# A first stage with maxima as b + relu(a - b) on row tiles, and a second attention with keys on partitions

## The reference

```
x = x + xattn(layernorm(x), ctx)      # ctx: 8192 keys; rope by position ids on q and k; softmax over 8192 keys
x = x + attn(layernorm(x))            # causal over the 512 latents; pairs (2i, 2i+1) rotated by position * frequency
x = x + moe(layernorm(x))             # 32 experts of 128, top 4 by softmax of the router, and 4 blocks of a shared expert
```

## Time and profile before

| | us |
|---|---|
| runs | 1833.15, 1833.43 and 1842.78; median 1833.43 |
| profiled execution | 1837.42, its span 1835.8, mean granted clock 0.965 |
| first stage, start to its last maximum | 0 to 726.2 |
| pass over all keys | 735 to 1316 |
| second attention's projections to its output projection | 1349.2 to 1501.6 |
| experts and the end | 1520 to 1835.8 |
| transfers, median from issue to landing | `kh<-kscr` 4.1, `qe<-vscr` 4.8, `cs<-kr` (swap) 6.3 |

### The profile page before, as it was taken

How to read it: one execution, slowest core, us unless ns; L and a number is a source line. 1 busy time by engine, 2 the same in 40 slices (tenths; PEclk the granted TensorE clock), 3 DMA queues, 4 the chain that set the end, 5 groups by cost and what they waited for, 6 DMA issues and landing times.

```text
span 1835.8 us, 21316 instructions
## 1 busy us (share of the span) xinstructions
PE 1686.4 (92%) x8556; PEld 1142.7 (62%) x8556; DVE 1357.2 (74%) x1095; ACT 839.8 (46%) x1083; POOL 686.4 (37%) x323
## 2 busy tenths in 40 slices
PE   5489999999999996998999999999985998999998
PEld 4377777777777773433444344434564986888886
DVE  5579899999999998999999898898752563222222
ACT  3312222222222210977888888888731654333332
POOL 3266655566665653998000000000040004444432
PEclk8789999999999998998999999999997999999999
DMA  4634445334445327543455545444339003343431
GB/s 150 202 115 149 154 165 164 126 126 149 150 168 161 106 92 190 138 115 93 111 120 123 120 118 124 115 115 115 96 95 265 20 1 115 122 131 122 132 121 57
DMA packets 73905, 231.62 MB, mean 126 GB/s; under 512 B 8924, under 2 KB 9180, under 8 KB 62992
## 3 DMA queue, kind: packets, MB, share of 16 engines
q1 hardware_dynamic: 72768, 227.39, 42.8%
q10 hardware_dynamic: 1040, 2.88, 0.6%
HBM read 150.45 MB, written 59.84 MB: 115 GB/s over the span
## 4 chain that ended last, share of the span: by engine, by line
PE 54%; POOL 17%; DVE 10%; DMA 8%; ACT 5%; issue 5%; SPq 1%; POOLq 0%; ACTq 0%; DVEq 0%
PE PS L585 12%; PE PS L617 10%; PE PS L113 8%; PE PS L114 8%; PE PS L115 7%; DMA cs<-kr 6%; POOL kr L453 4%; POOL cs L451 4%; POOL kr L450 4%; POOL kl L464 4%; PE PS L371 3%; DVE acc L608 2%; DVE mpart L375 2%; PE PS L893 2%; ACT P L591 2%
## 5 line engine op out<-in xcount | busy, mean ns | idle before, releaser
L375 DVE TENSOR_REDUCE mpart<-PS 128x2 f32<-128x1024 f32 x512 | 584.8, 1219 | 61.2 <-PE PS L371 61.1
L608 DVE TENSOR_TENSOR acc<-acc,P 128x2048 f32<-128x2048 f32 x216 | 508.5, 2417 | 34.9 <-ACT P L591 34.9
L591 ACT ACTIVATE P<-PS 128x1024 f32<-128x1024 f32 x512 | 481.5, 1039 | 97.8 <-PE PS L585 75.6
L371 PE MATMUL PS<-kh,Qbd 128*128 128x512 f32 x1024 | 326.5, 401 | 24.0 <-ACT kh L462 12.7
L617 PE MATMUL PS<-P,qe 128*32 128x512 f32 x2048 | 259.8, 606 | 0.7 <-ACT on L622 0.7
L371 PEld LDWEIGHTS PS<-kh,Qbd 128*128 128x128 f32 x1024 | 192.5, 192 | 81.9 <-DVE mpart L375 20.9
L108 POOL TENSOR_TENSOR w3l<-qk,w3h 128x2048 fp32r<-128x2048 f32 x2 | 9.1, 4557 | 481.7 <-ACT w3h L105 481.7
L108 POOL TENSOR_TENSOR El<-We,Eh 128x1536 fp32r<-128x1536 f32 x36 | 126.0, 3501 | 166.3 <-ACT Eh L105 166.3
L450 POOL TENSOR_TENSOR kr<-kr,cs 128x512 f32<-128x512 f32 x64 | 82.4, 1287 | 233.6 <-DMA cs<-kr 233.6
L1040 DVE TENSOR_TENSOR hf<-sg,PS 128x512 f32<-128x512 f32 x36 | 24.8, 688 | 193.2 <-PE PS L115 190.0
L438 ACT COPY cs<-PS 128x512 f32<-128x512 f32 x64 | 37.5, 587 | 240.0 <-PE PS L115 240.0
(11 more groups left out here) (206 smaller groups left out, 2785.1 us busy)
## 6 DMA issues: line engine op xcount, KB each, us to landing
kh<-kscr SPq DMA_DIRECT2D x129, 256.0 KB, 4.1
We<-in_w_e SPq DMA_DIRECT2D x36, 768.0 KB, 5.9
y<-in_y SPq DMA_DIRECT2D x16, 1024.0 KB, 4.8
cs<-kr SPq DMA_DIRECT2D x32, 512.0 KB, 6.3
vscr<-cs SPq DMA_DIRECT2D x16, 1024.0 KB, 4.3
kscr<-kh SPq DMA_DIRECT2D x16, 1024.0 KB, 4.3
kscr<-kl SPq DMA_DIRECT2D x16, 1024.0 KB, 4.3
qe<-vscr SPq DMA_DIRECT2D x64, 256.0 KB, 4.8
```

The lines of the kernel that those rows point to most:

```text
L371: ins = nc.tensor.matmul(PS[:, 2 * b + t, :], Qbd[:, h, qt * 128:(qt + 1) * 128], kh[c % 2][:, g, :], start=True, stop=True)
L375: maxfree[b] = DV.sig(nc.vector.tensor_reduce(mpart[:, 4 * (h % 4) + g, 2 * qp:2 * qp + 2, c], PS[:, 2 * b:2 * b + 2, :], AX, ALU.max))
L591: expm[s, pr] = spfree[b] = AC.sig(nc.scalar.activation(P[s % 4][:, 2 * pr:2 * pr + 2, :], PS[:, 2 * b:2 * b + 2, :], ACT.Exp, scale=SCALE))
L608: accm[s] = DV.sig(nc.vector.tensor_tensor(a[:, :, :], a[:, :, :], P[s % 4][:, :, :], ALU.add))
```

## The change

First stage: features are ordered by head, so a head's 32 rows are 32 neighbouring partitions, and four heads' score matmuls go to four row tiles. For keys a (first half of a chunk) and b (second half), max(a, b) = b + relu(a - b): `key_high` adds the difference of the halves to the high part (`khd`, 768 columns), the tiles make q·b and q·(a - b), ScalarE takes the relu of the second out of PSUM, VectorE adds and reduces in one operation. `kr` gets a second buffer; casts, ropes and maxima are laid on numbered slots (`at(unit, slot, ...)`, eight units of 12 slots a chunk), since `mm3` now calls `between` after every matmul. The units themselves stay, and `key_low` makes and writes the parts as before. `Qbd` goes.

```diff
-        Qbd = sb1("Qbd", [128, 16, 512], F32R)
+        khd = [sbt(f"khd{i}", [128, 4, 768], F32R) for i in range(2)]
+        kh = [x_[:, :, 0:512] for x_ in khd]
+        rel = [sb1(f"rel{i}", [128, 2, 2, 256]) for i in range(2)]
-        kr = sbx("kr", [128, 4, 512])
+        kr = [sbx(f"kr{i}", [128, 4, 512]) for i in range(2)]
         def swap(q, ln, dst, src):
-            ln.dma(q, dst[0:64, :, :], src[64:128, :, :])
-            return ln.dma(q, dst[64:128, :, :], src[0:64, :, :])
+            for r in range(0, 128, 32):
+                ln.dma(q, dst[r:r + 16, :, :], src[r + 16:r + 32, :, :])
+                m_ = ln.dma(q, dst[r + 16:r + 32, :, :], src[r:r + 16, :, :])
+            return m_
         def load_cs(c):
             if c < NCH:
-                SP.wait(rope_done.get(c - 2))
+                SP.wait(ropes_done.get(c - 2))
+                for r in range(0, 128, 32):
+                    csm[c] = l_cs[c % 2].dma(SP, cs[c % 2][r:r + 32, :, :],
+                                             cscr[c // 2, c % 2].rearrange("s f t n -> (s f) t n"))
+        def y_low(c):
+            PL.wait(yin[c], k_use.get(c - 2), yhm[c])
...
+            load_y(c + 1)
+        def rope(c):
+            SP.wait(kev[c], t_qrot, ropes_done.get(c - 1))
+            t_sw = swap(SP, l_sw, ks, kr[c % 2])
...
+            load_cs(c + 2)
+        def key_high(c, g):
+            x_ = khd[c % 2]
+            AC.wait(ropes[c][g], max_last.get(c - 2), kh_out.get(c - 2))
+            khm[c, g] = AC.sig(nc.scalar.copy(x_[:, g, 0:512], kr[c % 2][:, g, :]))
+            DV.wait(ropes[c][g], max_last.get(c - 2))
+            khd_m[c, g] = DV.sig(nc.vector.tensor_tensor(x_[:, g, 512:768], kr[c % 2][:, g, 0:256], kr[c % 2][:, g, 256:512],
+                                                         ALU.subtract))
+        def score_pairs(c, g, qp, which, left, right):
+            for t in range(2):
+                qt = 2 * qp + t
+                for hd in range(4):
+                    rows = slice(32 * hd, 32 * hd + 32)
+                    keys = slice(256, 512) if hd // 2 == which else slice(512, 768)
+                    o = PS[:, 2 * (left if hd // 2 == which else right) + hd % 2, t * 256:(t + 1) * 256]
+                    ins = nc.tensor.matmul(o, qh[rows, g, qt * 128:(qt + 1) * 128], khd[c % 2][rows, g, keys],
+                                           start=True, stop=True)
+            return PE.sig(ins)
+        def relu(i, b, m):
+            AC.wait(m)
+            return AC.sig(nc.scalar.activation(rel[i][:, :, :, :],
+                                               PS[:, 2 * b:2 * b + 2, :].rearrange("p j (t n) -> p j t n", t=2), ACT.Relu))
+        def larger(c, g, qp, hp, i, b, *marks):
+            DV.wait(*marks)
+            for j in range(2):
+                for t in range(2):
+                    m = DV.sig(nc.vector.tensor_tensor_reduce(
+                        out=rel[i][:, j, t, :], in0=PS[:, 2 * b + j, t * 256:(t + 1) * 256], in1=rel[i][:, j, t, :],
+                        scale=1.0, scalar=NEG, op0=ALU.add, op1=ALU.max,
+                        accum_out=mpart[:, 4 * (2 * hp + j) + g, 2 * qp + t, c:c + 1]))
+            return m
+        def maxima_1(c, i):
+            g, qp = i // 2, i % 2
+            r = [(cycle[0] + j) % 3 for j in range(3)]
+            PE.wait(t_qsplit, khm[c, g], khd_m[c, g], maxfree[r[0]], maxfree[r[1]])
+            m = score_pairs(c, g, qp, 0, r[0], r[1])
+            half[c, i] = r, relu(0, r[1], m)
+        def maxima_2(c, i):
+            g, qp = i // 2, i % 2
+            r, t_r = half.pop((c, i))
+            cycle[0] += 1
+            PE.wait(maxfree[r[2]], t_r)
+            max_last[c] = m = score_pairs(c, g, qp, 1, r[1], r[2])
+            maxfree[r[2]] = t_l = relu(1, r[2], m)
+            maxfree[r[1]] = larger(c, g, qp, 1, 0, r[1], m, t_r)
+            maxfree[r[0]] = larger(c, g, qp, 0, 1, r[0], t_l)
+        for c in range(NCH):
+            if c + 1 < NCH:
+                for k in range(4):
+                    at(8 * c + k, 4, y_high, c + 1, k)
+                at(8 * c + 3, 4, y_low, c + 1)
+            at(8 * c + 3, 11, rope, c)
+            for g in range(4):
+                at(8 * c + 8 + g, 8, key_high, c, g)
+            at(8 * c + 11, 11, key_low, c)
+            for i in range(8):
+                at(8 * c + 9 + i, 2, maxima_1, c, i)
+                at(8 * c + 9 + i, 7, maxima_2, c, i)
...
+                if u < 4:
+                    AC.wait(kl_m.get(c - 2))
+                    m = AC.sig(nc.scalar.activation(kr[c % 2][:, u, :], PS[:, 6 + b, :], ACT.Identity,
+                                                    bias=cst[:, 12 + u:13 + u]))
```

```diff
+        def rotate(part, g):
+            x, y_ = qk[part][:, g, :], xsw[part][:, g, :]
+            DV.wait(evs[part][g], t_cs2, t_xT)
+            a_ = DV.sig(nc.vector.stream_shuffle(y_, x, halves))
+            DV.wait(a_)
+            a_ = DV.sig(nc.vector.tensor_tensor(x, x, cs2[:, 0, g, :], ALU.mult))
+            b_ = DV.sig(nc.vector.tensor_tensor(y_, y_, cs2[:, 1, g, :], ALU.mult))
+            DV.wait(a_, b_)
+            rot[part, g] = DV.sig(nc.vector.tensor_tensor(x, x, y_, ALU.add))
...
+        def row_maxima(g, qt, hp, b):
+            PE.wait(hi[0, g], hi[1, g], pairfree[b], t_mkr)
...
+            pairfree[b] = mred[g] = DV.sig(nc.vector.tensor_reduce(
+                mxz[g % 2][:, qt, 64 * hp:64 * hp + 64:32], PS[:, 2 * b:2 * b + 2, 0:w], AX, ALU.max, negate=True))
+        def scores(g, j):
+            PE.wait(t_nmz[g], hl2[0, g], hl2[1, g], pairfree[0], pairfree[1])
+            for i, (kp_, qp_) in enumerate(((0, 0), (1, 0), (0, 1))):
+                for hd in range(4):
+                    nc.tensor.matmul(o[hd], QK[1][kp_][rows[hd], g, j * 128:(j + 1) * 128],
+                                     QK[0][qp_][rows[hd], g, 128 * j:512], start=i == 0, stop=False)
+            for hd in range(4):
+                nc.tensor.matmul(o[hd], onr[rows[hd], :], nmz[g % 2][rows[hd], 128 * j:512], start=False, stop=False)
+            for hd in range(4):
+                ins = nc.tensor.matmul(o[hd][:, 0:128], idr[:, :], mkr[:, 128:256], start=False, stop=True)
+                if hd % 2:
...
+        for g in range(4):
+            for j in range(4):
+                scores(g, j)
+                n = len(bursts) - 1
+                if j == 1 and g < 3:
+                    shifts(g + 1)
+                if g < 2:
+                    row_maxima(*late[g][2 * j], 2)
+                if n:
+                    values(n - 1)
+                if g < 2:
+                    row_maxima(*late[g][2 * j + 1], 2)
...
-        PE.wait(evk[0])
-        warm(72, 0)
-        t = transpose_split(lambda t_, c: at[:, t_, c * 128:(c + 1) * 128], R[0], R[1], list(t_at.values()), mk["e", nu - 1])
```

More of the change, by code:

```diff
@@ L112, in mm3 @@
             for k in range(nk):
[L113 to L117 removed]
+                for i, (a_, b_) in enumerate(((lh, rh), (lh, rl), (ll, rh))):
+                    ins = nc.tensor.matmul(o, a_(k), b_(k), start=first and k + i == 0,
+                                           stop=last and k == nk - 1 and i == 2)
+                    if between and k + i < nk + 1:
+                        between()
             return ins
@@ L485, in build @@
+        PL.wait(max_last[NCH - 2], kl_out[NCH - 1])
+        for i in range(2):
+            PL.sig(nc.gpsimd.memset(kp[i][96:97, :, :].bitcast(F32), 1.0))
         DV.wait(DV.last())
@@ new lines, in parts, with low_part @@
+        def parts(part, g):
+            AC.wait(rot[part, g])
+            hi[part, g] = AC.sig(nc.scalar.copy(QK[part][0][:, g, :], qk[part][:, g, :]))
+        def low_part(part, g):
+            DV.wait(hi[part, g], rot[part, g])
+            hl2[part, g] = DV.sig(nc.vector.tensor_tensor(QK[part][1][:, g, :], qk[part][:, g, :],
+                                                          QK[part][0][:, g, :].bitcast(F32), ALU.subtract))
+        rows = [slice(32 * hd, 32 * hd + 32) for hd in range(4)]
@@ L777, in build, with between_values @@
+        early = [(g, qt, hp) for g in range(2) for qt in (3, 2, 1, 0) for hp in range(2)]
+        def between_values():
+            if slots[0] >= 18 and slots[0] % 3 == 2 and early:
+                row_maxima(*early.pop(0), turn[0] % 2)
+                turn[0] += 1
+            slots[0] += 1
+        slots = [0]
         for part in range(3):
             PE.wait(t_ws[part], t_xT)
-            evs = []
+            evs[part] = []
             for u in range(4):
@@ L906, in build @@
+        values(15)
+        PE.wait(list(t_at.values()), t_wos)
         t_xT, _ = project(None, xn2, R[0], R[1])
```

443 lines of the change are left out of this document (179 added, 264 removed).

## The result

The changed kernel takes 1860.95 us (median of 4 runs, 1859.28 to 1865.55) against 1833.29 of the kernel before on the same chip: 1.0143 times as long, 95% interval 1.0104 to 1.0181. The prediction said 1715, with 1655 to 1830 as its range: the sign was wrong. The profiled execution has a span of 1858.0 us and a mean granted clock of 0.924 (before 0.965).

A forecast was written before the change was run, and what follows sets the result against it. TensorE (95% busy), VectorE (93%) and a GpSimd rope loop of 39.2 us a chunk were taken to bound the first stage. 1837.4 - 68 (first stage) - 50 (second attention) = 1719.4, less 4: 1715 us, range 1655 to 1830.

The forecast's parts named there:

- The swap stands behind the low part of the next y: 4.6 + 9 + 15.5 = 29 us in a row, covered by 35.: First stage, per chunk: low part of y, swap and rope take 29 us, hidden within a chunk of 35.2 us.
- ScalarE's queue, where a key cast that waits for its rope holds the evictions behind it: First-stage rival: rope or ScalarE's queue keeps a chunk at 39 us; 0 gained there, 1783 in all; chance 0.06.
- the differences, in VectorE's gap: First stage: four key differences of 256 columns a chunk fit into VectorE's idle gap, no time added.
- VectorE's ring: First stage, per unit: eight fused operations of 0.43 plus 0.65 of handing over to TensorE and back, 4.1 us.
- TensorE's ring: First stage, per unit: 12 projection matmuls of 0.2265, four tile groups of 0.14, 0.42 for changing over, 3.7 us.
- a price at all four changes: First stage: tiling-mode changes cost TensorE time both ways; its ring 4.1 instead of 3.7, unit nearer 4.55, 19 us later.
- The margin to 4.4: First stage: nearly equal rings in in-order queues miss the bound, so a unit of 4.1 becomes 4.4, 35.2 us a chunk.
- The accumulated output: First stage, VectorE's fused operation: 0.43 us taken, 0.36 if its accumulated output is free; rival 0.55, chance 0.17.
- Cheap maxima: First-stage rival: fused operation 0.36 us, unit 4.0, stage ends at 607 (-119), 1654 in all; chance 0.13.
- Values, late maxima and three of the four reciprocals lie beside that.: Second attention's loop: these run beside bursts of 3.7 to 1.7 us, so four groups take 43 us.
- goes on at its pace: Second attention: TensorE waits for VectorE at the third row maximum, then follows VectorE's pace; first burst at 1398.
- The rotation: Second attention, rotation on VectorE: 28 us, plus 3.4 beside GpSimd and 1.3 of waits, from 1353 to 1386.

The follow-up runs named there:

- Experiment 1: Changed kernel with the eight swap transfers issued on SP ahead of the next y load and the previous chunk's key writes: 1780.6 us, 0.9695 of the kernel before.
- experiment 3: Changed kernel with VectorE's key differences cut from 256 to 32 columns from chunk 2 on (wrong score maxima): 1858.5 us, 1.0116 of the kernel before.
- experiment 6: Experiment 1 with the key differences moved from VectorE to GpSimd: 1746.3 us, 0.9527 of the kernel before.
- experiment 4: Changed kernel with a VectorE shuffle in place of the swap transfers and the rope following by pieces: 1799.4 us, 0.9775 of the kernel before.
- experiment 5: Experiment 4 with the maxima five units behind the projection instead of nine: 1821.0 us, 0.9905 of the kernel before.
- experiment 7: Changed kernel with the swap as a VectorE shuffle, differences on GpSimd, maxima five units behind the projection: 1728.5 us, 0.9416 of the kernel before.
- experiment 8: Changed kernel with the second attention's 16 late row-maximum steps left out: 1843.4 us, 1.0029 of the kernel before.
- experiment 10: Changed kernel with filler matmuls at the second attention's 5.85 us wait: 50 calls 1857.7 us; 24 calls plus two ahead of each early maximum 1858.6 us.
- the mended first stage: The first stage of experiment 7, which took 1728.5 us in all without fillers in the second attention.
- experiment 9: Changed kernel with value and denominator products of each group's second and third key tile left out: 1875.4 us, 1.0218 of the kernel before.
- experiment 12: Experiment 7 with fillers in the second attention: 1714.3 us; also with shifts a burst earlier 1727.6 us, or with maxima four units behind 1712.6 us.
- the best version: Experiment 7 with fillers alone added in the second attention: 1714.3 us, 0.9353 of the kernel before.

## Why the prediction was wrong

**The first stage, the step that failed: "The swap stands behind the low part of the next y: 4.6 + 9 + 15.5 = 29 us in a row, covered by 35."** The row is 40.9. Left out was the low part of the keys, 4.8: it stands at the same slot as the rope, was entered a chunk earlier and so comes first on GpSimd and on SP. Too small were the swap, 13.5 instead of 9 (eight issues of 0.9 us), the rope, 16.0 instead of 15.5, and the gap of 1.6 that I had not. I had read the queues for what stands behind a waiting instruction and had not read what stands ahead of the one that counts. Experiment 1 changes that order alone and ends the stage 85 us earlier, of the 93 that were missing.

The mechanism was among the rivals, "ScalarE's queue, where a key cast that waits for its rope holds the evictions behind it", with a chance of 0.06. It was priced as if the worst were today's 39 us; nothing bounds a new loop by the old one.

**A second cause behind it: "the differences, in VectorE's gap"**, costed at nothing. They waited for GpSimd's instructions and took 0.42 to 3.73 us each. In the kernel as changed that was covered by the loop (experiment 3, 2.4 us); once the loop was cut it cost 34 us (experiment 6), and an innocent new schedule made it worse (experiments 4 and 5). Contention with GpSimd was in the rows (3.42 against 1.23), and I had used it for the rotation only.

**The rings of the first stage: the time right, the ring wrong.** The unit is 4.05 us, where 4.1 had been worked out for VectorE's ring; but it is TensorE's ring that sets it, forecast at 3.7. Its term for tiles and changing over was too small: 12 x 0.2265 leave 1.33 us of 4.05 for them, against 4 x 0.14 + 0.42 = 0.98 in the sum. Changing over showed on the way back too (0.34 instead of 0.23), where I had put nothing, so that the 4.1 that the prediction gave beside it for a price at all four changes was the nearer figure. VectorE's ring was too large: 8 x 0.345 and the 0.65 of handing over are 3.4, and its gap of 1.2 us is a wait for TensorE. That 4.05 and 4.1 agree is luck. The margin to 4.4 was not needed where nothing else held the units. Row tiles run together. The accumulated output costs no time: the Trainium skill (VectorE: DVE Perf Modes, "Two Vector instructions with no wait between them") calls such an operation two instructions, and the trace shows the two rows, but the second takes nothing from the next start, so that 0.36 could be had after all. "Cheap maxima" at 607 us, with a unit of 4.0, is close to what experiment 7 reaches, 616.6.

**The second attention, the step that failed: "Values, late maxima and three of the four reciprocals lie beside that."** They stand in TensorE's one queue between the bursts, 67.6 us busy of 83; leaving out the late maxima gives 17.5 (experiment 8). The second step: "goes on at its pace", and 4 us for the clock. The wait at the third row maximum came as said (5.85 us), but what followed ran at 0.50 of the clock, and the first burst came 17.5 us later than worked out. With fillers that hold the clock it comes 8 us earlier (58.3 in experiment 10); the other 9.5 stay. The rotation was right (33 worked out, 32.7 from 1376.79 to 1409.44), though one product of it took 5.11 us beside GpSimd, where the sum had given three of them 1.1 more each. The removed `warm(72, 0)` had been named, and priced at 4 us together with TensorE's waits; put back in a like form, fillers make the second attention 9.9 us shorter alone and 13.4 beside the mended first stage.

How the 33 us of the loop divide between order and clock is not shown: experiment 9 shows that they can't be parted by taking work away, since the clock answers. The traces have nearly the same loop at three clocks, though: 90.7 us at 0.69 (experiment 4), 82.6 at 0.81 and 77.2 at 0.92 (experiment 12). Carried on to 1.0 these give an estimate of 72 to 73 us, so that some 10 of the 33 us would be clock and the other 23 order. Experiment 4 also shows that one and the same code of the loop can differ by 8 us from one trace to the next. That the best version ends at the 1715 that I had forecast is chance: it has a first stage 42 us faster and a second attention 36 us slower than the sum (615.5 against 658; 135.8 against some 100).

## What to carry to other kernels

For a transfer that starts a chain, list everything that stands ahead of it in its queue, with what each of those waits for, and add up the loop until it closes; a busy share of 37% on GpSimd says nothing about such a loop. An operation moved to an engine takes that engine's conflicts along: ask which engine it was seen to wait for, what that one is doing at that moment, and for how long its longest instruction runs. Where TensorE waits often, price an edit only with the clock that the rows grant, and look where it falls before counting a gain.

## What the runs showed of the hardware that was not expected

- A transfer of 16 partitions, 128 KB, costs SP 0.7 to 1.4 us to issue (5.5 to 7.7 for eight, 4.7 to 5.7 for four), one of 1 MB mostly 0.36 to 0.58.
- Less work for TensorE can be slower: 1875.4 against 1861 us, with the clock at 0.57 instead of 0.81 over the loop.
- VectorE's shuffles (0.71 to 0.76 us, 64 of 512 columns) and its fused operations with one input in PSUM (0.345 from start to start) were not held by GpSimd beside them; the two-input difference out of SBUF was, up to 4.70 us (experiment 4) instead of 0.42.
- Eight row tiles of 256 columns take 0.43 us between plain matmuls, and each change between the two costs about 0.1.
